# A fused attention and expert kernel: the final stage works on pairs of batches

## The reference, cut to what matters

```python
# x: 8 batches x 256 tokens x 1024, float32
x = x + attention(linear_with_lora(x, W, b, lora_As, lora_Bs), w_q, w_k, w_v, w_o)
# per batch one of 8 matrices; per token the best 2 of 4 rank-16 experts
w = L0_cond2_weight[itok_B_3_7]                     # 8 x 1024 x 1024
h = einsum('bsi,boi->bso', x, w)
logits = h @ router_w.T;  gates = softmax(top-2 of logits, others -inf)
mid = einsum('tf,erf->ter', h, A)
delta = einsum('te,teo->to', gates, einsum('ter,eor->teo', mid, B) * 4.0)
x = x + delta
```

## Time and profile before

| | |
|---|---|
| three runs | median 1023.26 us (1022.05 to 1027.29) |
| profiled execution | 1027.09 us; its span 1024.9 us, mean granted TensorE clock 0.992 |
| TensorE busy | 996.2 us (97%) |
| VectorE, ScalarE, GpSimd busy | 639.2, 446.7, 235.4 us |
| attention's last matmuls | about 711 us into the span |
| batches 2 to 7 of the final stage | six windows from 770.47 to 1012.28 us |

### The profile page before, as it was taken

How to read it: one execution, slowest core, us unless ns; L and a number is a source line. 1 busy time by engine, 2 the same in 40 slices (tenths; PEclk the granted TensorE clock), 3 DMA queues, 4 the chain that set the end, 5 groups by cost and what they waited for, 6 DMA issues and landing times.

```text
span 1024.9 us, 17259 instructions
## 1 busy us (share of the span) xinstructions
PE 996.2 (97%) x6822; PEld 807.5 (79%) x6822; DVE 639.2 (62%) x1101; ACT 446.7 (44%) x786; POOL 235.4 (23%) x224
## 2 busy tenths in 40 slices
PE   7999999999899998999999999998999999999996
PEld 6878788777687776877768777785888889889886
DVE  6581822786846877467774688756565555655643
ACT  5121322355745657446664577737231332322321
POOL 1000001043422333224332256735010110011100
PEclk9999999999999999999999999999899999999998
DMA  7030311111411214111233233265766756856531
GB/s 269 0 103 1 134 47 55 42 44 38 126 45 39 54 49 126 36 43 49 59 115 90 81 106 110 79 219 190 213 210 200 227 193 199 246 192 192 194 124 41
DMA packets 49887, 117.40 MB, mean 115 GB/s; under 512 B 7298, under 2 KB 26114, under 8 KB 45712
## 3 DMA queue, kind: packets, MB, share of 16 engines
q1 hardware_dynamic: 40080, 81.70, 26.7%
q0 software_dynamic: 9728, 34.61, 11.0%
HBM read 86.38 MB, written 18.89 MB: 103 GB/s over the span
## 4 chain that ended last, share of the span: by engine, by line
PE 91%; DVE 3%; ACT 2%; DMA 1%; issue 1%; POOL 1%; SPq 0%
PE psP L818 20%; PE psW L1137 17%; PE psF L280 12%; PE psG L1165 8%; PE psO L909 6%; PE psS L885 5%; PE psT L896 5%; PE psX L1388 3%; PE psO L913 3%; PE psY L1407 2%; PE psP L840 2%; PE psF L291 2%; PE psP L842 1%; DVE q_stack L703 1%; PE psP L844 1%; PE psM L920 1%
## 5 line engine op out<-in xcount | busy, mean ns | idle before, releaser
L596 POOL TENSOR_TENSOR p_sum<-probs 128x512 f32<-128x512 f32 x128 | 169.8, 1327 | 342.1 <-ACT probs L645 342.1
L818 PE MATMUL psP<-x_hl,wq 128*128 128x512 f32 x960 | 236.8, 392 | 0.2 <-DVE v_sb L724 0.2
L734 DVE TENSOR_REDUCE nmax<-psS 128x2 f32<-128x512 f32 x256 | 164.5, 684 | 104.1 <-PE psS L885 99.2
L818 PEld LDWEIGHTS psP<-x_hl,wq 128*128 128x128 f32 x960 | 173.5, 188 | 31.1 <-DVE v_sb L724 0.4
L1137 PE MATMUL psW<-wq 128*128 128x256 f32 x1536 | 197.5, 285 | 0.0
L1137 PEld LDWEIGHTS psW<-wq 128*128 128x128 f32 x1536 | 191.5, 192 | 4.1 <-issue 0.2
L645 ACT ACTIVATE probs<-psT 128x512 f32<-128x512 f32 x256 | 139.0, 596 | 68.6 <-PE psT L896 67.7
L1146 ACT ACTIVATE cond_hi<-cond_raw 128x1024 fp32r<-128x1024 f32 x64 | 66.8, 1057 | 151.5 <-PE psG L1165 147.8
L1150 DVE TENSOR_TENSOR cond_lo<-cond_raw,cond_hi 128x1024 fp32r<-128x1024 f32 x64 | 78.6, 1239 | 82.3 <-ACT cond_hi L1146 82.2
L703 DVE TENSOR_TENSOR q_stack<-psP,q_stack 32x512 fp32r<-32x512 f32 x128 | 87.8, 686 | 11.4 <-ACT q_stack L610 9.6
L1093 POOL DMA_DIRECT2D cond_raw<-in_cond x64 | 33.9, 530 | 250.2 <-PE psG L1165 250.1
(11 more groups left out here) (128 smaller groups left out, 1298.5 us busy)
## 6 DMA issues: line engine op xcount, KB each, us to landing
cond_raw<-in_cond POOLq DMA_DIRECT2D x64, 512.0 KB, 4.1
x_raw<-in_xT SPq DMA_DIRECT2D x32, 256.0 KB, 3.3
q_stack<-q_stack SPq DMA_DIRECT2D x32, 256.0 KB, 2.9
o_scratch<-o_sb SPq DMA_DIRECT2D x64, 128.0 KB
o_raw<-rden_scratch SPq DMA_DIRECT2D x32, 256.0 KB, 5.1
o_raw<-o_scratch SPq DMA_DIRECT2D x8, 1024.0 KB, 8.8
x_sb<-in_xT SPq DMA_DIRECT2D x8, 1024.0 KB, 6.2
outT<-x_sb SPq DMA_DIRECT2D x32, 256.0 KB, 2.5
```

Source lines behind the costliest of these rows:

```text
L596: pool.tensor_tensor(p_sum[:, heads], probs[:, 0, heads], probs[:, 1, heads], ALU.add).then_inc(sum_done, 1)
L734: dve.tensor_reduce(nmax[:, n % 2, 2 * hp:2 * hp + 2, qt], psS[:, i % 2].rearrange("p (h k) -> p h k", h=2), AX.X, ALU.max, negate=True).t ...
L818: mm = pe.matmul(out, wq[:, i, w, k * P:(k + 1) * P], x[:, k, part], start=(k == 0 and n_ == 0), stop=False)
```

## The change

Batches 0 and 1 keep tiles of 256 columns (`one_tile`). Batches 2 to 7 are projected in pairs: x and o of two batches lie side by side, and `pair_tile` runs 24 matmuls of 512 columns for both; its residual is one add of 512. Only the last pair's tile 7 is done as two halves (`half_tile`). The experts of a pair are added during the next pair, also with 512 columns, so batch 0's no longer stand in batch 1. The two middles of a pair follow each other. The copies to g_t move from VectorE to ScalarE, behind the next batch's first two cond_hi, and odd batches turn G in psY. Gates take 6 waited steps instead of 11. At the end, middle(6), half_tile(1), turn_g(7) and middle(7) follow each other; batch 6's experts run in four PSUM banks beside batch 7's gates, and are copied by ScalarE, added by GpSimd and stored by SP in an order written out. x is loaded and stored in tiles of both batches (eight DMAs of 256 KB in pieces of 1 KB, where one of 1 MB and four of 256 KB were), and o lands in pieces of 1 KB. The loads of o for batches 2 and 3 have memory of their own and no wait for TensorE.

```diff
-    CH = 11
...
     def load_o(sp, n):
-        if n >= 2:
-            sp.wait_ge(wo_done, KT * (n - 1))
+        if n >= 4:
+            sp.wait_ge(wo_done, tile(n // 2 - 1, 0))
         sp.wait_ge(before.rden_stored, 16 * (n // 2 + 1))
         for h in range(HG):
-            sp.dma_start(rden_land(n % 2)[HD * h:HD * h + HD], rden_scratch[n, h:h + 1].to_broadcast([HD, G, T])
+            sp.dma_start(rden_land(n)[HD * h:HD * h + HD], rden_scratch[n, h:h + 1].to_broadcast([HD, G, T])
                          ).then_inc(o_landed[n % 2], 16)
-        sp.dma_start(o_land(n % 2), oT[n]).then_inc(o_landed[n % 2], 16)
-        sp.dma_start(x_sb[:, n % 2], xT[n]).then_inc(x_landed[n % 2], 16)
+        sp.dma_start(o_land(n), oT[n]).then_inc(o_landed[n % 2], 16)
+    def load_x(sp, p, m):
+        sp.dma_start(x_tile(p, m), xT[2 * p:2 * p + 2, :, m].rearrange("b p t -> p b t")).then_inc(x_landed[m], 16)
...
+        load_o(sp, 2)
+        before.store_rden(sp, PAIRS - 1)
+        load_o(sp, 3)
+        for m in range(KT):
+            if m == 6:
+                sp.wait_ge(fb_lo_done, 1)
+            load_x(sp, 1, m)
+        for p in range(1, PAIRS):
+            if p < LASTP:
+                for n in (2 * p + 2, 2 * p + 3):
+                    load_o(sp, n)
+            store(p - 1)
+            if p < LASTP:
+                sp.wait_ge(stored, 16 * KT * p)
+                for m in range(KT):
+                    load_x(sp, p + 1, m)
+        for n, j in ((B - 2, 0), (B - 2, 1), (B - 2, 2), (B - 1, 0), (B - 2, 3), (B - 1, 1), (B - 1, 2), (B - 1, 3)):
+            if n == B - 2:
+                sp.wait_ge(z_added, j + 1)
+            else:
+                sp.wait_ge(y_added, KT * LASTP + j + 1)
+            store_two(n, j)
...
+        for j in range(YT):
+            pool.wait_ge(z_copied, j + 1)
+            x = x_two(LASTP, j)[:, :, 0]
+            pool.tensor_tensor(x, x, y_sb[j][:], ALU.add).then_inc(z_added, 1)
...
+    def w_o_tile(pe, i, m, o, n, ks=range(KT)):
+        out = psW[:, i % 2, 0:n]
+        if ks[0] == 0 and i >= 2:
+            pe.wait_ge(x2_done, i - 1)
...
+    def pair_tile(pe, p, m, ks=range(KT)):
+        w_o_tile(pe, tile(p, m), m, lambda part, k: two(o_split[p % 2][:, part, k]), T2, ks)
+    def half_tile(pe, c):
+        w_o_tile(pe, HALF + c, KT - 1, lambda part, k: o_split[LASTP % 2][:, part, k, c], T)
...
+        def second():
+            gates(0)
+            for m in range(KT):
+                if m < 6:
+                    cond_row_hi(act, KT + m + 2)
+                if m == 3:
+                    scale_hi(act, 2)
+                if m == 5:
+                    scale_hi(act, 3)
+            copy_g(1)
+            for r in range(2):
+                cond_row_hi(act, ROWS + r)
+            turn_copies(1)
+            gates(1)
+        def pair(p):
+            a, b = 2 * p, 2 * p + 1
+            for m in range(KT - 1):
+                if m < 2:
+                    gated_part(a - 2 + m)
+                if m == 3:
+                    copy_g(a)
+                for r in range(2 * m + 2, 2 * m + 4):
+                    cond_row_hi(act, ROWS * p + r)
+                if m == 3:
+                    turn_copies(a)
+                if p < LASTP and m in (2, 4):
+                    scale_hi(act, a + 2 if m == 2 else b + 2)
+            copy_g(b)
+            if p < LASTP:
+                for r in range(2):
+                    cond_row_hi(act, ROWS * (p + 1) + r)
+                turn_copies(b)
+                gates(a)
+                gates(b)
...
+        gates(B - 2)
+        turn_copies(B - 1)
+        gated_part(B - 2)
+        gates(B - 1)
+        copy_y(0)
+        copy_y(1)
+        gated_part(B - 1)
+        copy_y(2)
+        copy_y(3)
+    def z_bank(j):
+        return psY[:, j] if j < 2 else psW[:, j - 2]
+    def last_bank(j):
+        return psG[:, j] if j < 2 else psY[:, j - 2]
...
+            dve.wait_ge(mid_done, n + 1)
+            dve.tensor_reduce(top[:], middle[:, :, ER:EC], AX.X, ALU.max)
+            step(dve.tensor_copy(mid[n % 2][:], middle))
+            dve.tensor_tensor(shift[:], logit, top[:].unsqueeze(2).to_broadcast([P, 2, E]), ALU.subtract).then_inc(shifted, 1)
+            for i in range(E):
+                if i:
+                    ins = dve.tensor_tensor(beats[:, :, i, 0:i], logit[:, :, 0:i], logit[:, :, i:i + 1].to_broadcast([P, 2, i]),
+                                            ALU.is_lt)
+                if i < E - 1:
+                    ins = dve.tensor_tensor(beats[:, :, i, i + 1:E], logit[:, :, i:i + 1].to_broadcast([P, 2, E - 1 - i]),
+                                            logit[:, :, i + 1:E], ALU.is_ge)
             step(ins)
-            step(dve.tensor_tensor(beats[:], beats[:], later[:].unsqueeze(1).to_broadcast([P, 2, E - 1, E]), ALU.mult))
-            dve.tensor_reduce(wins[:], beats[:], AX.X, ALU.add)
             step(dve.tensor_reduce(losses[:], beats[:].rearrange("p t i j -> p t j i"), AX.X, ALU.add))
-            step(dve.tensor_tensor(losses[:, :, 0:E - 1], losses[:, :, 0:E - 1], wins[:], ALU.subtract))
-            step(dve.tensor_tensor(losses[:], losses[:], chosen[:].unsqueeze(1).to_broadcast([P, 2, E]), ALU.is_lt))
-            dve.wait_ge(gate_exp, n)
-            step(dve.tensor_tensor(gate[:], gate[:], losses[:], ALU.mult))
+            dve.wait_ge(gate_exp, n + 1)
+            step(dve.scalar_tensor_tensor(gate[:], losses[:], 1.5, gate[:], ALU.is_lt, ALU.mult))
             step(dve.tensor_reduce(gsum[:], gate[:], AX.X, ALU.add))
             step(dve.reciprocal(gsum[:], gsum[:]))
-            step(dve.tensor_tensor(gate[:], gate[:], wide(gsum[:]), ALU.mult))
+            assert done[0] == CH
...
+        def pair(p):
+            a, b = 2 * p, 2 * p + 1
+            for m in range(KT - 1):
+                residual(dve, tile(p, m))
+                if m < 2:
+                    gated_part(a - 2 + m)
+                for r in range(2 * m + 2, 2 * m + 4):
+                    cond_row_lo(dve, ROWS * p + r)
+                if 2 <= m < 6:
+                    add_y(p - 1, 2 * m - 4)
+                    add_y(p - 1, 2 * m - 3)
+                if p < LASTP and m in (1, 2):
+                    normalise(dve, a + m + 1)
+                if p < LASTP and m in (5, 6):
+                    scale_lo(dve, a + m - 3)
+            residual(dve, tile(p, KT - 1))
+            if p < LASTP:
+                for r in range(2):
+                    cond_row_lo(dve, ROWS * (p + 1) + r)
+                gates(a)
+                gates(b)
+        first()
+        second()
+        for p in range(1, PAIRS):
+            pair(p)
+        gates(B - 2)
+        residual(dve, HALF + 1)
+        gated_part(B - 2)
+        gates(B - 1)
+        gated_part(B - 1)
         for j in range(YT):
-            add_y(B, j)
+            add_last(j)
...
+        def second():
+            cond_row(pe, KT)
+            for m in range(1, KT - 1):
+                one_tile(pe, 1, m)
+                cond_row(pe, KT + m)
+            cond_row(pe, KT + 7)
+            one_tile(pe, 1, KT - 1, range(4))
+            turn_g(1)
+            one_tile(pe, 1, KT - 1, range(4, KT))
+            middle(1)
+        def pair(p):
+            a, b = 2 * p, 2 * p + 1
+            pe.wait_ge(o_lo_done, b + 1)
+            for m in range(KT - 1):
+                if m == 4:
+                    pair_tile(pe, p, m, range(4))
+                    turn_g(a)
+                    pair_tile(pe, p, m, range(4, KT))
+                else:
+                    pair_tile(pe, p, m)
+                cond_row(pe, ROWS * p + 2 * m)
+                cond_row(pe, ROWS * p + 2 * m + 1)
+                if m < 2:
+                    turn_gated(a - 2 + m)
+                elif m < 6:
+                    y_tile(p - 1, 2 * m - 4)
+                    y_tile(p - 1, 2 * m - 3)
+            if p < LASTP:
+                pair_tile(pe, p, KT - 1, range(4))
+                cond_row(pe, ROWS * p + 14)
+                cond_row(pe, ROWS * p + 15)
+                pair_tile(pe, p, KT - 1, range(4, KT))
+                turn_g(b)
+                middle(a)
+                middle(b)
         first()
-        for n in range(1, B):
-            batch(n)
-        turn_gated(B)
+        second()
+        for p in range(1, PAIRS):
+            pair(p)
+        half_tile(pe, 0)
+        cond_row(pe, ROWS * LASTP + 14)
+        cond_row(pe, ROWS * LASTP + 15)
+        middle(B - 2)
+        half_tile(pe, 1)
+        turn_g(B - 1)
+        middle(B - 1, range(1))
+        turn_gated(B - 2)
+        middle(B - 1, range(1, 2))
         for j in range(YT):
-            y_tile(B, j)
+            y_two(B - 2, j, z_bank(j), z_done)
+        turn_gated(B - 1)
+        for j in range(YT):
+            if j >= 2:
+                pe.wait_ge(z_copied, j - 1)
+            y_two(B - 1, j, last_bank(j), y_done)
```

(72 more changed lines are left out.)

323 lines of the change are left out of this document (133 added, 190 removed).

## The result

The changed kernel takes 1016.97 us (median of 7 runs, 1016.45 to 1021.24) against 1025.8 for the kernel before on the same chip (7 runs, 1022.05 to 1028.31). The ratio of the means is 0.9928, interval 0.991 to 0.9946: 7.4 us faster, where 10.3 were forecast (the medians lie 8.8 apart). The time is above the forecast of 1013.0 and inside its range, which went to 1018.5. The profiled execution took 1016.79 us, its span is 1015.1.

What follows compares the result with a forecast made beforehand. TensorE, busy for 97% of the span, was taken as the bound. The terms -2.1 - 0.7 + 0.6 - 5.0 - 1.3 - 1.8 = -10.3 us, from the median 1023.26, gave 1013.0 us, range 1009.5 to 1018.5.

Steps and rivals of the forecast that it cites:

- Joined tiles: Wo tiles and experts in pairs 1 and 2: 512-column matmuls, 5.45 us a tile, saving 5.0 us.
- Rival C: Joining matmuls saves only 2.5 ns a time, so the kernel takes 1018.8 us; chance 4%.
- Experts a pair behind: Batch 1 no longer carries batch 0's turning and experts: 2.1 us less before pair 1.
- g_t on ScalarE: g_t copies leave VectorE: 0.7 us saved ahead of middle(0), 0.6 us of wait added for batch 1.
- The last pair: Up to the end of middle(7): 2.2 us less by joining, but one turning and a wait more; net -1.3 us.
- E: The moment middle(7), the last batch's middle product, ends; times at the kernel's end are counted from it.
- rival D: Transfers in 1 KB pieces take twice the time and come late, about 1022 us; chance 8%.
- The end: From the end of middle(7) to the end of the kernel: 10.8 us against 12.6, -1.8 us.
- An end set by GpSimd or SP: Sign of a wrong prediction: GpSimd or SP sets the kernel's end later than 8 us after middle(7).
- The base: Starting time 1023.26 us, the median of the runs, taken as free of the half-clock stretch costing 3.4 us.
- rival A: Shorter waits ahead of the 68-column products make the clock fall: 1016.4 us for one fall, 1019.8 for two; chance 17%.
- Rival B: The clock falls halfway into each of three doubled middles, making the kernel slower, 1031 us; chance 4%.

Runs made afterwards that it cites:

- split end: Changed kernel, batch 6's quarters 0 and 1 added by VectorE from PSUM, 2 and 3 by GpSimd after the gates: 0.9895 of the kernel before, median 1015.46 us.
- early end: On the split end, quarters 2 and 3 of batch 6 multiplied between middle(7)'s halves, VectorE adding all four: 0.9916 of the kernel before, median 1015.8 us.

## Why the prediction came out as it did

- **Joined tiles, right.** 5.46 us against 5.45, a pair 78.17 against 78.1; undone, it costs 7.0 us where 6.6 were worked out. Rival C falls.
- **Experts a pair behind and g_t on ScalarE, right in sum.** From middle(0) to pair 1 it saved 1.5 us as forecast; the wait ahead of middle(1) showed as 0.2 us and a slower start of the product, not 0.6. The 0.7 us at middle(0) was right.
- **The last pair up to E, right:** 79.35 us, 1.26 less, forecast 1.3. The pairs had no other wait, and 1 KB pieces made none: rival D falls.
- **The end, wrong.** Forecast E + 10.8, -1.8 us; measured E + 15.2, +2.6. The step that failed is the one that let GpSimd's adds run beside the gates at no cost, and with it the term that 2.8 us lie between the last issue and the end. Three things took its place:
  - The gated values are ready 1.8 us late. 1.6 of it is the wait for GpSimd's adds, shown by two runs; the rest is the new form of the four instructions, 0.88 us undisturbed instead of 0.64. With SP's queue and the half clock behind them, the last issue starts at E + 9.9 instead of 8.0.
  - The last store lands 3.7 us after its issue instead of 2.4, 1.3 us more, with 1 MB more of stores going out just before it. Leaving them out of the split end took 0.9 us away. In the early end, where half of them go out before the gates and the last adds come slower, nothing was left of it.
  - The end waits for GpSimd's DRAIN, 1.2 us more than the 0.4 that otherwise lie behind the landing. Leaving the adds out took such a wait away, 1.6 us, in a variant of the split end.

  Together, 1.9 + 1.3 + 1.2 = 4.4 us; the sizes are read from the changed kernel's profile. An end set by GpSimd or SP was one of the prediction's own signs of being wrong. I had no bound for the first, although the kernel before already shows the effect the other way round: the earlier trace rows has GpSimd adds of 1288 ns in the median and one of 3134. In the trace that one starts at 690.89 us, while VectorE's `normalise` with its two SBUF inputs runs from 690.59 to 692.88, and it ends 1.1 us after it, as if most of it had come behind.
- **The base, wrong.** I took the half-clock stretch for an exception and started from 1023.26, the median of three runs, which happened to be low: over more runs the medians are 1025.6 to 1026.65, and in the last series 16 of 22 executions have a mean clock of 0.993 or less. That most of them have this stretch is likely and not shown, since the mean doesn't place it. Without the stretch the change is worth 8.3 - 2.6 = 5.7 us by the profiles; the 7.4 measured probably have in them that it is rarer after the change (the copies alone were worth 3.2 us in the kernel before, 2.5 more than their wait). I had listed it only as a danger (rival A), with the waits' lengths as the argument, and that argument was right the other way round: a wait cut from 1.20 to 0.53 us took the fall away. So it is partly luck that the time lies inside the range: the end took 4.4 us more than forecast and the base was 2.5 us too low, and a gain by the clock that the sum didn't contain made up for part of both.
- **Rival B didn't come:** the doubled middles run at 1.00 throughout.

## What to carry to other kernels

Before an elementwise step is handed to GpSimd because it is idle, look at what VectorE does at that moment: products of two SBUF tensors stand still while it adds, and if it is the last thing GpSimd does, the program ended no sooner than 6.6 us after it in any profile here. At the end of a kernel count the bytes that are still to be stored, not only the last instruction; and at a short wait ask what the clock does after it, for that can be worth more than the wait.

## What the runs showed of the hardware that I had not expected

- GpSimd's closing DRAIN ends 6.6 to 6.7 us after its last work in the nine profiles where that was an add or a memset. After a DMA issue it was 6.6 us in two profiles of the kernel before and 7.4 to 7.5 in three others.
- A matmul with fp32r operands costs its columns at 2.4 GHz and about 13 ns, at 256 columns (119.6 ns) as at 512 (227).
- 0.76 us of TensorE's waiting ahead of middle(0)'s 68-column products was followed by the 1.2 GHz level for several us, 0.53 us in none of nine profiles; one profile stayed at full clock after 1.20 us.
